# Second attention with 64-column values, transposed heads and an output product of its own

## The chip, the cores and the metric

The kernel runs on one core of one Trainium2 chip. The metric is the device time of one execution in microseconds, median of several runs.

## The reference, cut to what matters

Two layers, each a cross-attention and a feed-forward part, on 32 batches of 128 tokens by 128 features. All four are fused into one kernel. The change is in the second attention:

```
x = x + tanh(g_xattn[1]) * L1_xattn(layernorm(x), ctx)
def L1_xattn(x, context, Wq, Wk, Wv, Wo, bo):      # H = 16 heads, DH = 64
    q = (x @ Wq).reshape(b, n, H, DH)
    k = (context @ Wk * SCALE).reshape(b, m, H, DH)
    v = (context @ Wv).reshape(b, m, H, DH)
    attn = softmax(einsum('bihd,bjhd->bhij', q, k))
    out = einsum('bhij,bjhd->bihd', attn, v).reshape(b, n, H * DH)
    return out @ Wo + bo
```

Behind it a mixture of 8 experts takes each token to the expert with the largest logit (top 1).

## The kernel before, in words

There are five parts, in blocks with a barrier between them: setup, first attention, first FFN, second attention, second FFN. Every instruction of every engine stands in an order written out by hand; engines meet at semaphores. The second attention goes over the 32 batches in a software pipeline: `step(n)` scores and weighs batch n and at the same time projects batch f = n + 1. Batches 0 and 1 are written out, the other 30 are a loop over pairs (`Fori(1, PAIRS)`).

Value and output weights are folded: for each head, `fold` (L789) multiplies Wv of that head (128x64) with Wo of that head (64x128) to a 128x128 matrix, kept in float16 as a high and a low part (`k.M_hi`, `k.M_lo`, written at L683 and L459). In step(n) TensorE does:

- `project` (L1557 to L1566): q and k, four times 12 float16 products of 128 columns into `l_qk_bank`;
- `project_context` (L1568 to L1583): Z = ctx times M, four times three products of 512 columns into `l_tz`; ScalarE copies each to `l_Z` (L1499), where a head has 128 columns and a column of ones;
- `score_by_query` (L1585, tile `l_a`) for the maxima, `transpose_maxima` (L1601), `score_by_key` (L1603, tile `l_b`) for the shifted scores, of which ScalarE takes the exponentials (`l_probs`, L1494);
- `weigh` (L1636 to L1651): eight times two heads, each float32 product with the 128x128 probabilities as the stationary operand and 129 columns of Z moving, into `l_pv`;
- VectorE (`sums`, L1143) takes the reciprocal of the last column and adds each head's 128 columns, scaled, to x or to `l_acc`.
- GpSimd (`pair`, L1432) normalises batch n + 2, adds the bias, makes the low parts of q and k (`rests`, L1424), adds x and `l_acc` to `l_rows` (`rows_out`, L1416) and scatters the rows of two batches to their experts (`scatter`, L1409).

The router's small steps for the pair before (`route_transpose`, `route_logits`, `route_ranks`, `choose`, `put`) lie between these. The bank `l_tz` is one PSUM bank that Z and the transposed x share.

## Time and profile before

| | us |
|---|---|
| median of 3 runs | 820.46 (819.62 to 821.15) |
| the profiled execution's own time | 819.96 |
| its span | 818.2 |
| setup, first attention and first FFN | 0 to 294.5 |
| second attention, from its first product to the last router transposes | 294.5 to 708.5 |
| rest of the routing and second FFN | 708.5 to 818.2 |

The profile is of one execution; 1.8 us of its time lie outside the span. A row of the timeline has a start, a duration, the engine, the line, the operation, and what it writes and reads. Matmuls are pipelined: a duration is a latency, and what a group costs is the distance from its start to the start of the next group. PEld is the load of the stationary operand, PE the product. A float32 product is two instructions, each with a load of its own, so a count of x4 in the weighing is two heads.

### The profile page before, as it was taken

To read this page: it belongs to the slowest core of one execution; us is meant where nothing else is said; L and a number is where in the kernel's file an instruction comes from. 1 tells how busy PE (TensorE), PEld (TensorE's weight loads), DVE (VectorE), ACT (ScalarE), POOL (GpSimd) and SP (SyncE) were. 2 spreads that over 40 slices of the span, in tenths; PEclk is the share of its full clock that TensorE was granted. 3 is DMA by queue.
4 is the path that set the end of the run, shared out by engine and by line. 5 is a ranking of instruction groups with operands and counts; after the bars stand their busy time and mean duration, and the time that the engine had idled before them with its cause. 6 is when DMAs were issued, how large, how long until landed. Compare 5 with 4: busy or idle time off the path is not lost. (4 is left out here: it accounts for less than half of the span.)

```text
span 818.2 us, 30776 instructions
## 1 busy us (share of the span) xinstructions
PE 777.2 (95%) x10683; PEld 637.6 (78%) x10683; DVE 622.3 (76%) x2406; ACT 557.8 (68%) x1125; POOL 475.8 (58%) x892
## 2 busy tenths in 40 slices
PE   3999999999999989999999999999999999979995
PEld 2777777777788858888888888888888888558884
DVE  4799999998777766888888888888888888734442
ACT  1688888886455557777777777777777777447772
POOL 6645777772011155586676776776776776604554
PEclk9999999999999999999999999999999999999998
DMA  8804999800200000000000000000000000023100
GB/s 215 309 3 150 265 246 236 184 1 3 72 1 0 0 1 2 3 7 7 7 0 7 7 7 7 3 3 7 7 7 7 0 7 7 10 67 87 38 30 21
DMA packets 56160, 41.65 MB, mean 51 GB/s; under 512 B 3900, under 2 KB 51654, under 8 KB 55859
## 3 DMA queue, kind: packets, MB, share of 16 engines
q1 hardware_dynamic: 52400, 36.39, 17.6%
q0 software_dynamic: 2272, 4.27, 1.6%
q10 hardware_dynamic: 1440, 0.40, 0.4%
q8 instruction: 27, 0.44, 0.2%
q14 instruction: 21, 0.15, 0.1%
HBM read 18.07 MB, written 23.44 MB: 51 GB/s over the span
## 5 line engine op out<-in xcount | busy, mean ns | idle before, releaser
L1650 PE MATMUL l_pv<-l_Z,l_probs 128*128 128x129 f32 x1024 | 164.1, 284 | 0.5 <-DVE l_acc L1159 0.5
L1650 PEld LDWEIGHTS l_pv<-l_Z,l_probs 128*128 128x128 f32 x1024 | 138.4, 191 | 20.1 <-DVE l_acc L1159 4.9
L1430 POOL TENSOR_TENSOR l_qk_lo<-w,l_qk_hi 128x512 f16<-128x512 f32 x132 | 148.8, 1159 | 0.8 <-ACT l_qk_hi L1510 0.8
L1159 DVE SCALAR_TENSOR_TENSOR x_sb<-l_pv,l_inv,x_sb 128x128 f32 (+1 forms) x256 | 89.8, 351 | 35.3 <-DVE l_inv L1146 6.9
L52 PE MATMUL l_tz<-M,cT 128*128 128x512 f16 x396 | 107.3, 380 | 0.0
L1494 ACT ACTIVATE l_probs<-l_b 128x512 f32<-128x512 f32 x128 | 72.8, 595 | 50.6 <-PE l_b L1616 50.5
L1484 ACT ACTIVATE w<-l_qk_bank 128x512 f32<-128x512 f32 x129 | 77.0, 597 | 43.8 <-PE l_qk_bank L52 42.1
L520 DVE TENSOR_REDUCE n_shared<-fold_bank 128x4 f32<-128x512 f32 x128 | 87.3, 682 | 9.5 <-PE fold_bank L735 9.4
L1136 DVE TENSOR_REDUCE l_neg_max<-l_a 128x4 f32<-128x512 f32 x132 | 85.9, 682 | 2.3 <-PE l_a L1594 1.8
L1488 ACT ACTIVATE l_qk_hi<-w 128x512 f16<-128x512 f32 x129 | 80.5, 624 | 1.0
L1499 ACT ACTIVATE l_Z<-l_tz 128x512 f32<-128x512 f32 x128 | 76.6, 599 | 3.6
L1159 DVE SCALAR_TENSOR_TENSOR l_acc<-l_pv,l_inv,l_acc 128x128 f32<-128x128 f32 x224 | 76.6, 342 | 0.0
L365 POOL TENSOR_TENSOR n_rstd<-n_var,n_half 128x4 f32<-128x4 f32 x20 | 20.2, 1008 | 87.9 <-DVE n_var L359 87.8
L378 POOL TENSOR_TENSOR l_work<-l_stats,l_work 128x1 f32<-128x1 f32 x67 | 12.6, 189 | 79.8 <-DVE l_stats L497 45.6
L1146 DVE RECIPROCAL l_inv<-l_pv 128x2 f32<-128x2 f32 x256 | 40.6, 159 | 20.4 <-PE l_pv L1650 19.9
L52 PE MATMUL l_qk_bank<-cT,w_hi 128*128 (+1 forms) x528 | 55.0, 219 | 0.1
L52 PEld LDWEIGHTS l_tz<-M,cT 128*128 (+1 forms) x396 | 34.5, 98 | 19.8
L52 PE MATMUL l_qk_bank<-l_T_hi,w_hi 128*128 128x128 f16 x268 | 48.7, 220 | 0.2 <-DVE l_T_lo L1130 0.2
L52 PE MATMUL l_qk_bank<-l_T_hi,w_lo 128*128 128x128 f16 x268 | 48.3, 219 | 0.0
L52 PE MATMUL l_qk_bank<-l_T_lo,w_hi 128*128 128x128 f16 x268 | 48.3, 219 | 0.0
L652 ACT ACTIVATE l_stack<-fold_bank 128x512 f16<-128x512 f32 x64 | 39.0, 610 | 13.1 <-PE fold_bank L52 13.1
L52 PE MATMUL l_qk_bank<-cT,w_lo 128*128 (+1 forms) x264 | 47.6, 219 | 0.0
(276 smaller groups left out, 2265.3 us busy)
## 6 DMA issues: line engine op xcount, KB each, us to landing
expert_rows<-empty_row SPq DMA_DIRECT2D x8, 2178.0 KB, 24.4
x_sb<-expert_rows SPq DMA_DIRECT2D x36, 66.0 KB, 2.3
x_sb<-in_x SPq DMA_DIRECT2D x4, 512.0 KB, 6.9
ctx_sb<-in_ctx SPq DMA_DIRECT2D x4, 512.0 KB, 8.2
w<-in_L_ffn_w SPq DMA_DIRECT2D x1, 2048.0 KB, 9.3
w_raw<-in_L_ffn_gate_w SPq DMA_DIRECT2D x1, 1408.0 KB, 9.2
w_raw<-in_L_ffn_up_w SPq DMA_DIRECT2D x1, 1408.0 KB, 11.5
downT<-in_L_ffn_down_w SPq DMA_DIRECT2D x2, 512.0 KB, 4.2
```

The lines of the kernel that those rows point to most:

```text
L52: last = nc.tensor.matmul(out, lhsT, rhs, start=start and n == 0, stop=stop and n == len(pairs) - 1, skip_group_check=True)
L520: nc.vector.tensor_reduce(neg_max[:, s % 2, G * r:G * r + 4], a_bank[r % 2][:, :].rearrange("p (j n) -> p j n", j=4), AX.X, ALU.max, negat ...
L652: nc.scalar.activation(stack[:, s % DEEP, m].rearrange("p j n -> p (j n)"), stack_bank[:, :], ACT.Copy).then_inc(ready, 1)
L1136: nc.vector.tensor_reduce(neg_max[:, at:at + Q], a_bank[half][:, :].rearrange("p (t n) -> p t n", t=Q), AX.X, ALU.max, negate=True).then_i ...
L1146: nc.vector.reciprocal(inv[:, 2 * m:2 * m + 2], O[:, :, P]).then_inc(inv_ready, 1)
L1159: nc.vector.scalar_tensor_tensor(out=total, in0=O[:, h, 0:P], scalar=inv[:, j:j + 1], in1=total, op0=ALU.mult, op1=ALU.add).then_inc(summe ...
L1430: nc.gpsimd.tensor_tensor(qk_lo[:, w, m, Q * u:Q * u + Q].rearrange("p t n -> p (t n)"), qk[:, u, m, :], qk_hi[:, w, m, Q * u:Q * u + Q].r ...
L1484: nc.scalar.activation(qk[:, u, m, :], qk_bank[:, :], ACT.Copy).then_inc(qk_ready, 1)
L1488: nc.scalar.activation(qk_hi[:, w, m, Q * u:Q * u + Q].rearrange("p t n -> p (t n)"), qk[:, u, m, :], ACT.Copy)\
L1494: nc.scalar.activation(probs[:, at:at + Q, :].rearrange("p h n -> p (h n)"), b_bank[half][:, :], ACT.Exp, scale=float(HD1) ** -0.5).then_i ...
L1499: nc.scalar.activation(Z[:, w, Q * q:Q * q + Q, 0:P], tz_bank[:, :].rearrange("p (h n) -> p h n", h=Q), ACT.Copy)\
L1650: last = nc.tensor.matmul(pv_bank[m % 2][:, h * (P + 1):(h + 1) * (P + 1)], probs[:, 2 * m + h, :], Z[:, w, 2 * m + h, :], start=True, sto ...
```

## The change

- Nothing is folded. Wv (columns in another order of heads) and Wo (rows in the same order) are each split by GpSimd into two float16 parts, `k.vo_hi` and `k.vo_lo`, during the first FFN (16 pairs of small operations). The fold's products, copies and subtractions go.
- V = ctx times Wv has 64 columns a head, so that `project_context` runs twice a batch and not four times; `l_V` has 65 columns a head.
- `weigh` runs four times with four heads of 65 columns.
- VectorE divides four heads at once (`sums`, one reciprocal and one product) into a tile `l_heads`.
- New: `transpose_heads`, twice a batch four float32 transposes into `l_tz`; `heads_hi` (ScalarE) and `heads_lo` (VectorE) make float16 parts; `project_heads`, 24 float16 products of 128 columns into `l_qk_bank`; `acc_out` (VectorE) scales the sum.
- The loops are gone, all 32 steps are written out, and the last ones leave out the work for batches that don't exist (the loop did it on padding). In step 0 the maxima are transposed ahead of the first projection. At the start, two results go to banks of their own.
- The routing is spread by `late`, `middle` and `early` over three steps, and `l_rows` and `l_slot_i` have two buffers.

The diff, cut to its core:

```diff
-    for t, name in ((k.wvT, "L1_xattn_Wv"), (k.wo1, "L1_xattn_Wo")):
-        sp.dma_start(t[:, :, :], A[name].rearrange("(j p) n -> p j n", p=P)).then_inc(k.late_landed, 16)
+    sp.dma_start(k.vo_raw[:, 0:H // 2, :].rearrange("p j n -> p (j n)"), A["L1_xattn_Wv"]).then_inc(k.late_landed, 16)
+    sp.dma_start(k.vo_raw[:, H // 2:H, :], A["L1_xattn_Wo"].rearrange("(j p) n -> p j n", p=P)).then_inc(k.late_landed, 16)
...
-                def fold(u):
-                    for t in range(4):
-                        for half in range(2):
-                            some = slice(HD1 * half, HD1 * half + HD1)
-                            last = nc.tensor.matmul(k.fold_bank[2 * u + half][:, t * P:t * P + P], k.wvT[some, 4 * u + t, :], k.wo1[some, 4 * u + t, :],
-                                                    start=True, stop=True, tile_position=(HD1 * half, 0))
-                    last.then_inc(k.folded, 1)
...
+                def split_late(n):
+                    raw, hi, lo = (t[:, bass.ds(n, 1), :].rearrange("p a n -> p (a n)") for t in (k.vo_raw, k.vo_hi, k.vo_lo))
+                    nc.gpsimd.tensor_copy(hi, raw).then_inc(k.vo_hi_ready, 1)
+                    pool.wait_ge(k.vo_hi_ready, n + 1)
+                    nc.gpsimd.tensor_tensor(lo, raw, hi, ALU.subtract).then_inc(k.vo_lo_ready, 1)
...
+                def sums(n, m):
+                    O = pv_bank[m % 2][:, 0:SIDE].rearrange("p (h n) -> p h n", h=Q)
+                    some = slice(Q * m, Q * m + Q)
+                    dve.wait_ge(pv_done, 4 * n + m + 1)
+                    nc.vector.reciprocal(inv[:, some], O[:, :, HD1]).then_inc(inv_ready, 1)
+                    dve.wait_ge(inv_ready, 4 * n + m + 1)
+                    nc.vector.tensor_tensor(heads[:, some, :], O[:, :, 0:HD1],
+                                            inv[:, some].rearrange("p (h a) -> p h a", a=1).broadcast_to([P, Q, HD1]), ALU.mult).then_inc(heads_ready, 1)
+
+                def heads_lo(n, part):
+                    some = slice(Q * part, Q * part + Q)
+                    dve.wait_ge(OT_hi_ready, 2 * n + part + 1)
+                    nc.vector.tensor_tensor(OT_lo[:, some, :].rearrange("p j n -> p (j n)"), tz_bank[:, :],
+                                            OT_hi[:, some, :].rearrange("p j n -> p (j n)"), ALU.subtract).then_inc(OT_lo_ready, 1)
+
+                def acc_out(n):
+                    dve.wait_ge(out_done, n + 1)
+                    dve.wait_ge(x_done, n + 1)
+                    nc.vector.tensor_scalar(acc[:, n % 2, 0:P], qk_bank[:, 0:P], k.tg[:, 1:2], None, ALU.mult).then_inc(acc_ready, 1)
...
-                    for h in range(2):
-                        last = nc.tensor.matmul(pv_bank[m % 2][:, h * (P + 1):(h + 1) * (P + 1)], probs[:, 2 * m + h, :],
-                                                Z[:, w, 2 * m + h, :], start=True, stop=True)
+                    for h in range(Q):
+                        last = nc.tensor.matmul(pv_bank[m % 2][:, h * (HD1 + 1):(h + 1) * (HD1 + 1)], probs[:, Q * m + h, :],
+                                                V[:, n % 2, Q * m + h, :], start=True, stop=True)
                     last.then_inc(pv_done, 1)
+
+                def transpose_heads(n, part):
+                    pe.wait_ge(heads_ready, 4 * n + 2 * part + 4)
...
+                    for t in range(Q):
+                        pair = slice(2 * (Q * part + t), 2 * (Q * part + t) + 2)
+                        last = nc.tensor.transpose(tz_bank[:, t * P:t * P + P], heads[:, pair, :].rearrange("p h n -> p (h n)"), k.ident[:, :])
+                    last.then_inc(OT_moved, 1)
+
+                def project_heads(n):
+                    pe.wait_ge(OT_lo_ready, 2 * n + 2)
+                    if n + 2 < B:
+                        pe.wait_ge(qk_ready, 4 * n + 12)
+                    elif n + 1 == B:
+                        pe.wait_ge(acc_ready, n)
+                    pairs = []
+                    for t in range(H // 2):
+                        hi, lo, w_hi, w_lo = OT_hi[:, t, :], OT_lo[:, t, :], k.vo_hi[:, H // 2 + t, :], k.vo_lo[:, H // 2 + t, :]
+                        pairs += [(hi, w_hi), (lo, w_hi), (hi, w_lo)]
+                    both_products(nc, qk_bank[:, 0:P], pairs).then_inc(out_done, 1)
...
+                def step(n):
+                    f, u, w = n + 1, n % 2, 1 - n % 2
+                    if n == 0:
+                        transpose_maxima(n)
+                    if f < B:
+                        project(f, 1, 0)
+                    if n:
+                        transpose_maxima(n)
+                        weigh(n - 1, 3)
                     score_by_key(n, u, 0)
+                    if f < B:
+                        score_by_query(f, w, 0)
+                        project_context(f, 0)
+                        project(f, 0, 1)
+                    weigh(n, 0)
+                    if n:
+                        transpose_heads(n - 1, 1)
+                    if f < B:
+                        project(f, 1, 1)
+                    weigh(n, 1)
                     score_by_key(n, u, 1)
+                    if f + 1 < B:
+                        transpose(f + 1, u)
+                    if n:
+                        project_heads(n - 1)
+                    if f < B:
+                        score_by_query(f, w, 1)
+                        project_context(f, 1)
+                    if f + 1 < B:
+                        project(f + 1, 0, 0)
+                    weigh(n, 2)
+                    transpose_heads(n, 0)
```

On TensorE, the second half of step 1 stood like this in the kernel before (`l_pv` weighing, `l_b` scores by key, `l_a` scores by query, `l_tz` the shared bank; the twelve products of a projection are left out at the first dots, and after the second ones):

```order
L1650 MATMUL l_pv<-l_Z,l_probs 128x129 x2
L1611 MATMUL l_b<-l_neg_maxT,pick_half 128x128 x8
...
L1616 MATMUL l_b<-l_qk_lo,l_qk_hi 128x128 x8
L1594 MATMUL l_a<-l_qk_hi 128x128 x8
L52 MATMUL l_tz<-M,cT 128x512 x3
L1650 MATMUL l_pv<-l_Z,l_probs 128x129 x2
L52 MATMUL l_qk_bank<-l_T_hi,w_hi 128x128
...
L52 MATMUL l_tz<-M,cT 128x512 x3
L1650 MATMUL l_pv<-l_Z,l_probs 128x129 x2
```

and stands like this in the changed one, up to the end of the step:

```order
L1677 MATMUL l_pv<-l_V,l_probs 128x65 x4
L1631 MATMUL l_b<-l_neg_maxT,pick_half 128x128 x8
...
L1636 MATMUL l_b<-l_qk_lo,l_qk_hi 128x128 x8
L1565 MATMUL l_tz<-ident,l_xn 128x128
L53 MATMUL l_qk_bank<-vo,l_OT_hi 128x128
L53 MATMUL l_qk_bank<-vo,l_OT_lo 128x128
...
L1614 MATMUL l_a<-l_qk_hi 128x128 x8
L53 MATMUL l_tz<-vo,cT 128x512 x3
...
L1677 MATMUL l_pv<-l_V,l_probs 128x65 x4
L1694 MATMUL l_tz<-ident,l_heads 128x128 x4
```

Of the two groups of Z products one is left; the output product of the batch before (24 instructions) and four transposes have come in, and the weighing stands in larger groups. An x2 or x4 of a float32 product here is of heads, two instructions each in the trace.

On GpSimd, the end of a pair stood so in the loop: the scatter of the pair before, then the two additions to `l_rows`.

```order
L1430 TENSOR_TENSOR l_qk_lo<-w,l_qk_hi 128x512
L1396 TENSOR_TENSOR l_taker<-l_taker 128x1
L1414 DMA expert_rows<-l_rows,l_slot_i 35456x132 x2
L1395 ISA
L1396 TENSOR_TENSOR l_taker<-l_taker 128x1
...
L1422 TENSOR_TENSOR l_rows<-x_sb,l_acc 128x132
...
L1422 TENSOR_TENSOR l_rows<-x_sb,l_acc 128x132
```

Now one addition stands ahead of the scatter in an even step, and one in an odd step (an even step and the beginning of the odd one):

```order
L1415 TENSOR_TENSOR l_qk_lo<-w,l_qk_hi 128x512 x2
L1380 TENSOR_TENSOR l_taker<-l_taker 128x1
L1407 TENSOR_TENSOR l_rows<-x_sb,l_acc 128x132
L1380 TENSOR_TENSOR l_taker<-l_taker 128x1
L1398 DMA expert_rows<-l_rows,l_slot_i 35456x132 x2
L1415 TENSOR_TENSOR l_qk_lo<-w,l_qk_hi 128x512 x2
```

Behind the last step the scatter of pair 14 stands ahead of the addition of batch 31 in both.

## Rows read from the trace of the kernel before

**Rows 1.** Page, busy us, share of the span, instructions

```profile
PE 777.2 (95%) x10683; PEld 637.6 (78%) x10683; DVE 622.3 (76%) x2406; ACT 557.8 (68%) x1125; POOL 475.8 (58%) x892
```

**Rows 2.** Busy time by stage: window, length, each engine busy (instructions), granted clock

```profile
320.43:332.26 11.83, 11.83 (x178) 10.20 (x175) 9.39 (x34) 9.25 (x18) 7.12 (x12) 1.00 0.02 4
332.26:344.89 12.63, 12.63 (x183) 10.78 (x181) 10.08 (x42) 9.45 (x18) 7.20 (x13) 1.00 0.01 2
344.89:357.07 12.18, 12.18 (x183) 10.34 (x181) 10.28 (x45) 9.06 (x17) 8.44 (x14) 1.00 0.01 3
357.07:692.21 335.14, 335.14 (x4850) 285.42 (x4848) 276.57 (x1160) 250.07 (x460) 237.06 (x408) 1.00 0.02 6
692.21:708.47 16.26, 14.99 (x189) 11.53 (x186) 12.38 (x53) 10.74 (x19) 10.92 (x20) 1.00 0.03 9
```

**Rows 3.** Timeline of TensorE, batch 1: start, duration, what, count

```profile
320.43 0.28 PE L1601 MATMUL l_a<-ident,l_neg_max 128*128 128x128 f32 x1
320.54 0.61 PE L1650 MATMUL l_pv<-l_Z,l_probs 128*128 128x129 f32 x4
320.99 0.81 PE L52 MATMUL l_tz<-M,cT 128*128 128x512 f16 x3
321.64 0.61 PE L1650 MATMUL l_pv<-l_Z,l_probs 128*128 128x129 f32 x4
322.18 0.40 PE L1611 MATMUL l_b<-l_neg_maxT,pick_half 64*128 64x128 bf16 x8
...
323.08 0.39 PE L1594 MATMUL l_a<-l_qk_hi 64*128 64x128 f16 x8
323.40 0.23 PE L52 MATMUL l_qk_bank<-l_T_hi,w_hi 128*128 128x128 f16 x1
...
324.08 0.66 PE L1650 MATMUL l_pv<-l_Z,l_probs 128*128 128x129 f32 x4
324.58 0.81 PE L52 MATMUL l_tz<-M,cT 128*128 128x512 f16 x3
```

**Rows 4.** Timeline of TensorE, products with 8 moving columns, batches 15 and 16

```profile
492.22 0.48 PE L1627 MATMUL l_pv<-routerT,l_rowsT 128*128 128x8 f32 x3
492.33 0.37 PE L1627 MATMUL l_pv<-routerT,l_rowsT 128*128 128x8 f32 x2
492.56 0.69 PE L1650 MATMUL l_pv<-l_Z,l_probs 128*128 128x129 f32 x4
...
498.61 0.22 PE L52 MATMUL l_pv<-l_onehot,l_ones 128*128 128x8 bf16 x3
498.69 0.69 PE L1650 MATMUL l_pv<-l_Z,l_probs 128*128 128x129 f32 x4
```

**Rows 5.** Waits of weight loads, 320 to 704 us: total, times, longest

```profile
PEld l_pv L1650 <- DVE l_acc L1159: 4.2, 15, 0.3
```

**Rows 6.** Page, groups of instructions: busy, mean ns, idle before

```profile
L1159 DVE SCALAR_TENSOR_TENSOR l_acc<-l_pv,l_inv,l_acc 128x128 f32<-128x128 f32 x224 | 76.6, 342 | 0.0
L1499 ACT ACTIVATE l_Z<-l_tz 128x512 f32<-128x512 f32 x128 | 76.6, 599 | 3.6
```

**Rows 7.** Timeline around the fold, TensorE and VectorE

```profile
199.34 1.16 PE L793 MATMUL fold_bank<-wo,wvT 64*128 64x128 f32 x16
...
205.61 0.74 DVE L459 SCALAR_TENSOR_TENSOR M<-fold_bank,tg,M 128x512 f16<-128x512 f32 x1
```

**Rows 8.** Timeline of TensorE ahead of batch 0

```profile
303.80 0.40 PE L1594 MATMUL l_a<-l_qk_hi 64*128 64x128 f16 x8 [0.27 <-ACT l_qk_hi L1510]
...
309.49 0.28 PE L1601 MATMUL l_a<-ident,l_neg_max 128*128 128x128 f32 x1
```

**Rows 9.** Timeline of GpSimd, last scatter in the loop

```profile
702.67 0.19 POOL L1396 TENSOR_TENSOR l_taker<-l_taker 128x1 f32<-128x1 f32 x1 [1.22 <-DVE l_slot_i L1232]
...
704.74 0.96 POOL L1414 DMA_INDIRECT expert_rows<-l_rows,l_slot_i  x1 [0.30 <-issue]
707.11 0.33 POOL L1396 TENSOR_TENSOR l_taker<-l_taker 128x1 f32<-128x1 f32 x2 [1.40 <-DMA expert_rows<-l_rows,l_slot_i]
```

More of the change, by code:

```diff
@@ L40 @@
 WARM_UP = 8
+HEAD_ORDER = [2 * (4 * u + t) + half for u in range(2) for half in range(2) for t in range(4)]
 SPLIT = 2 * E * I1 + 2 * H * HD1
@@ L1328, in _ @@
+                sums(B - 1, 3)
+                ranks_out(PAIRS - 2)
+                put(PAIRS - 2, 0)
+                heads_lo(B - 1, 1)
+                for part in range(1, 4):
+                    put(PAIRS - 2, part)
+                acc_out(B - 1)
                 j = PAIRS - 1
@@ L1455, in _ @@
                 pool.wait_ge(primed, 6)
-                pool.wait_ge(summed, 4)
+                pool.wait_ge(heads_ready, 2)
                 for u in range(2):
                     bias(u, 4 + u)
-                rests(0, 0, first=True)
-                pair(0)
+                for u in range(2):
+                    rests(0, u, first=True)
+                for n in range(4):
+                    step(n)
                 pool.wait_ge(k.rows_cleared, 16 * (E + 1))
-                pool.wait_ge(row_primed, 1)
-                with pool.Fori(1, PAIRS) as i:
-                    pair(i, i - 1)
+                for n in range(4, B):
+                    step(n)
+                scatter(PAIRS - 2)
+                rows_out(B - 1)
                 deviations(PAIRS - 1)
@@ L1532, in _ @@
-                        z_out(f, w, 2)
+                    for half in range(2):
+                        exponentials(n, 1, half)
+                    if f < B:
+                        v_out(f, 1)
+                    if f + 1 < B:
                         projected(f + 1, 0, 0)
-                        z_out(f, w, 3)
                         projected_hi(f + 1, u, 0, 0)
+                for n in range(B):
+                    step(n)
+                for part in range(2):
+                    heads_hi(B - 1, part)
@@ L1717, in _ @@
+                project_heads(B - 1)
                 pe.wait_ge(exp_done, 4 * B + 4)
```

509 lines of the change are left out of this document (239 added, 270 removed).

## Prediction, made before the changed kernel was run

> **What bounds the kernel now.** Start with the page: TensorE is busy for 95% of the span [rows 1], which may mean little, since its ends are modelled. So the stage the change touches is read next, by windows that run from one transpose of the maxima (L1601) to the next, which is one step of the second attention [rows 2]. A step takes 11.83 us in batch 1, 12.63 and 12.18 in batches 2 and 3, and 335.14 us for the next 27, 12.41 each. In each window TensorE is busy without a gap at the full granted clock, while VectorE is busy for 10.3 us and ScalarE for 9.4 at the most. The waits of the weight loads say the same: the longest kind adds up to 4.2 us over some 380 us [rows 5]. So the second attention goes at the pace at which TensorE can issue, and what is to be priced is the distance from one TensorE group to the next, which is in the timeline of batch 1 [rows 3]:
>
> - a projection of 12 products of 128 columns: 323.40 to 324.08, 0.68 us, mostly 0.67; 0.056 each
> - three products of 512 columns: 320.99 to 321.64, 0.65
> - scores by key 0.90 (322.18 to 323.08), by query 0.32 (to 323.40)
> - a float32 transpose 0.11 (320.43 to 320.54)
> - weighing two heads, four instructions: 0.45 behind other float32 work (320.54), 0.54 ahead of the scores by key (321.64), 0.50 behind a projection (324.08); so 0.112 an instruction, and 0.055 or 0.09 for the change of kind.
>
> With 4 projections (2.68), 4 groups of 512 columns (2.60), 2 of each score (1.81 and 0.64), 2 transposes (0.22) and 8 weighings (3.87) the sum is 11.82, and the trace has 11.83: the price list is complete.
>
> **The weighing.** This is the term on which all rests. The product gets 65 columns for 129. At 129 columns an instruction takes 0.112 us, as much as 258 columns take at 2.4 GHz, so 65 columns would need 0.057. But the stationary operand, 128x128 in float32, is loaded anew for each. The router's product has such an operand and only 8 moving columns: its instructions start at 492.22 and 492.33, and the next group comes at 492.56, two more further on: 0.112 each [rows 4]. The same with a bfloat16 operand takes 0.025 (three from 498.61 to 498.69) [rows 4]. So 0.112 is what the float32 load costs, at 8 as at 129 columns, and I take 0.112 at 65. The bounds are 0.057 and 0.112. The Trainium skill has both sides, on the page "TensorE: Matmul & The Clock Gate": the section "Back-to-back issue gap" lets the moving columns alone set the gap, by which this would come out at the 0.057 bound; the section "LDWEIGHTS (loading the stationary operand)" lets the load take its columns over 1.2 GHz, about 107 ns, whatever moves. The trace sides with the second.
>
> What is left of a gain is the grouping: four groups of 8 instructions at 0.112 are 3.58, with three changes behind a projection (0.165) and two ahead of the scores (0.18) 3.92. Before: 3.87. Nothing is gained.
>
> **The rest of a step.** Z to V takes away two groups of 512 columns: 1.30 off. The heads' transposes are 8 times 0.11: 0.88 on. The output product is 24 times 0.056: 1.34 on. The transpose of x now stands behind the scores by key instead of a weighing; a full-width group behind tiled ones costs more there, some 0.1 to 0.2 (the last gap of scores by query in front of a projection), 0.14 taken. With weighing +0.05 that is +1.11: a plain step of 12.93 us. For the 24 products the page's section "Back-to-back issue gap" also has about 81 ns an instruction in a real stream of loads and products with 128 columns; by it they would cost 0.6 more a step and the sum would be 19 us higher. The twelve in 0.67 say 0.056.
>
> Routing costs TensorE 12.63 - 11.83 = 0.80 in an even step and 0.35 in an odd one [rows 2], 0.57 on average, of which about 0.15 is waiting for VectorE's sums [rows 5]; that wait goes, since VectorE now does a batch's sums in 8 instructions for 24. So 0.42 stays, and a full step takes 13.35 for 12.41.
>
> **Do the others keep up?** ScalarE has two copies of values less and two of transposed heads more, all of 0.60 [rows 6]: the same load. VectorE loses 16 additions of 0.34 [rows 6] and gets two subtractions of 512 columns (0.74 each, as the fold's [rows 7]), four products of 256 columns and one of 128, under 0.74 each: no more than before. The bank `l_tz` is used in turn by V, heads, x, V, heads; with a product 0.65 or 0.45, a copy 0.60 and a subtraction 0.74 and the latencies, the ring is some 8.7 us, inside 13.3. A step walked through from its first projection (0), with TensorE's groups at the distances above: scores by key end at 2.7, so the exponentials are there at 3.5 and 4.0 and `weigh(n, 0)` at 4.3 finds them; the heads transposed at 5.3 to 5.7 are copied by 6.5 and subtracted by 7.3, needed at 8.4 by the transpose of x and at 8.5 by the output product; that one ends at 9.9, `acc_out` at 10.4 at the latest, needed at 10.8 by the projection that takes its bank; ScalarE has the second float16 part of k at 9.5 in a plain step (9.9 with logits, when TensorE is later too), needed at 9.8 by the scores by query; the heads transposed at the end of the step are ready 2.0 into the next, needed at 3.0. So each wait finds its producer done; the tightest margins are 0.2 to 0.4. On GpSimd `rows_out` now comes some 11.4 into each step, just ahead of the router's transposes, and in even steps the scatter (3.0 us) follows it; behind it queue the low parts of q and k for the step after the next, which have a step of slack.
>
> **The steps.** From L1601 of batch 1 to that of batch 31 before: 371.78 us [rows 2]. Now: 12.93, then 13.15 and 13.32 in batches 2 and 3, in which not all routing has begun, 26 steps of 13.35 (347.1), and 11.8 for batch 30, where the projections for a batch that doesn't exist are left out. Together 398.3: +26.5.
>
> **The edges.** (1) The fold goes: two bursts of 1.09 us, 199.34 and again 3.7 us later, hidden for two thirds, and VectorE's subtraction from 205.61 to 206.35 behind which the block ended [rows 7]: -1.4 (0 to -2.5). (2) Ahead of batch 0 the second scores by query start at 303.80 and the maxima are transposed at 309.49 [rows 8], behind two groups of Z, filler products, a second transpose and two projections. In the new order they wait only for VectorE's maxima (two of 0.68), and the first x part comes earlier, as it no longer waits behind the second copy: about 303.7, with the projection that was ahead of it now behind; at the first scores by key this is -5.6 (-4 to -6.5). From there to L1601 of batch 1 the lists before and after have the same length (10.0). (3) At the end: from L1601 of batch 31 to the router's transposes 16.26 before [rows 2]. Now the last weighing is followed by transposes, copy, subtraction, output product and scaling; and GpSimd has the scatter of pair 14 ahead of the last rows, which takes 3.0 us (702.67 to 705.70 [rows 9]). `put` for it is done about 13.9 us in, so the rows are ready at 17.6: +1.4 (0 to +3). (4) GpSimd's 16 splits lie in the first FFN, where it is idle most of each 5 us: 0 (to +2, if they slow VectorE).
>
> **Sum.** 26.5 - 1.4 - 5.6 + 1.4 = +20.9. Against the profiled execution's own 819.96 that is 840.9; this is 0.5 under the median of the runs, and I say 841.
>
> **Rivals.**
> - *The load is no floor* (65 columns take 0.057): 32 instructions times 0.055 are 1.76 a step, 56 us less in all, though ScalarE and VectorE (10 us busy each, in order) would not let a step fall below some 11.6; about 790. For it: the arithmetic of columns. Against it: 8 columns take as long as 129. Below some 0.09 an instruction it would turn the result: 0.02 times 32 times 30 is 21 us. Chance 0.05: faster. The skill's section on the issue gap, quoted above, is this rival's rule.
> - *New waits.* The chain from the transposes through ScalarE and VectorE back to `l_tz`, or `acc_out` before the next projection, comes late by 0.3 to 0.6 a step, as the margins above are only estimates: 30 steps make 9 to 18, so 850 to 859. The same if written-out code had to be fetched late; but batch 1 was written out before, and its step has no gap. Chance 0.13.
> - *Part of the grouping pays more than I count*, and the 0.14 and the routing's 0.2 go too: 0.4 a step less, 829. Chance 0.10.
> - The chance of my own case, 834 to 848, is 0.72.
>
> A measurement tells 0.2% (1.6 us) from no change. Faster: 0.06; within it: 0.01; slower: 0.93. The range that holds 8 in 10: 831 to 851.
>
> **What will show it.** Right: L1601 to L1601 at 13.2 to 13.4 us with TensorE still without gaps; PEld rows of the weighing at 0.112 distance with 65 columns; 24 output products in 1.34; waits of PEld still short. Wrong: weighing instructions closer than 0.1 (first rival); idle time of PEld in front of `l_tz<-ident,l_heads`, `l_qk_bank<-vo` or the projections (second); a first transpose of the maxima later than 305.

## The result: 3 per cent slower, as the price list of TensorE had it

| | before | changed |
|---|---|---|
| median | 820.04 us (819.04 to 821.15, 4 runs) | 844.95 us (841.57 to 848.15, 4 runs) |
| profiled execution | 819.96 us, span 818.2 | 845.78 us, span 844.1 |

The ratio is 1.0305, 95% interval 1.028 to 1.0331. The forecast was 841, range 831 to 851. The two profiled executions differ by 25.8 us. Here is where they lie, each stage between two TensorE instructions that both traces have:

| stage | before | changed | difference | forecast |
|---|---|---|---|---|
| last scores of the first attention to the first hidden product of the first FFN | 11.63 | 11.51 | -0.1 | -1.4 |
| last transpose of that FFN to the first product of the second attention | 2.34 | 3.41 | +1.1 | 0 |
| from there to the transpose of the maxima of batch 1 | 25.90 | 22.04 | -3.9 | -5.6 |
| to that of batch 31 | 371.78 | 396.79 | +25.0 | +26.5 |
| to the router's last transposes | 16.26 | 20.47 | +4.2 | +1.4 |
| all the rest | | | -0.4 | 0 |

The steps make 25 of the 26 us. The four stages that are edges were forecast at -5.6 together and came out at +1.3; the steps were forecast 1.5 too high. Each column is one execution. The end above all differs between profiles: with the same instructions in it (in one of them with fewer moving columns) it takes 19.1, 20.5 and 23.1 us in three of them; run 6 has more on this.

### The profile page after: what moved, and what is told of

It is laid out like the page before. It is cut to its first block and busy times, and to the rows that moved or that the text cites. A ratio compares the mean times of both kernels' runs of the same rounds, so it can differ in the third digit from the quotient of the medians.

```text
span 844.1 us, 29663 instructions
## 1 busy us (share of the span) xinstructions
PE 796.6 (94%) x11374; PEld 677.0 (80%) x11379; DVE 589.0 (70%) x1972; ACT 546.4 (65%) x1107; POOL 481.9 (57%) x907
## 5 line engine op out<-in xcount | busy, mean ns | idle before, releaser
L1677 PE MATMUL l_pv<-l_V,l_probs 128*128 128x65 f32 x1024 | 134.9, 275 | 0.5 <-DVE l_rowsT L1156 0.5
L1677 PEld LDWEIGHTS l_pv<-l_V,l_probs 128*128 128x128 f32 x1024 | 124.4, 192 | 0.7 <-issue 0.7
L1497 ACT ACTIVATE l_OT_hi<-l_tz 128x512 f16<-128x512 f32 x64 | 38.2, 597 | 39.6 <-PE l_tz L1694 38.4
L1140 DVE TENSOR_TENSOR l_heads<-l_pv,l_inv 128x256 f32<-128x256 f32 x128 | 54.3, 424 | 4.4
L53 PE MATMUL l_tz<-vo,cT 128*128 128x512 f16 x192 | 52.5, 383 | 0.0
L53 PE MATMUL l_qk_bank<-cT,w_hi 128*128 128x128 f16 x504 | 52.5, 219 | 0.0
L53 PE MATMUL l_qk_bank<-vo,l_OT_hi 128*128 128x128 f16 x512 | 49.4, 222 | 1.4 <-DVE l_OT_lo L1146 1.4
L1146 DVE TENSOR_TENSOR l_OT_lo<-l_tz,l_OT_hi 128x512 f16<-128x512 f32 x64 | 43.9, 685 | 9.2 <-ACT l_OT_hi L1497 7.1
L1897 POOL DMA_INDIRECT out<-f_result,f_token x39 | 38.5, 988 | 13.9 <-issue 10.2
L53 PE MATMUL l_qk_bank<-vo,l_OT_lo 128*128 128x128 f16 x256 | 45.6, 222 | 0.0
## 6 DMA issues: line engine op xcount, KB each, us to landing
w_raw<-in_L_ffn_up_w SPq DMA_DIRECT2D x1, 1408.0 KB, 11.6
```

What stands on the lines that cost most here:

```text
L53: last = nc.tensor.matmul(out, lhsT, rhs, start=start and n == 0, stop=stop and n == len(pairs) - 1, skip_group_check=True)
L1140: nc.vector.tensor_tensor(heads[:, some, :], O[:, :, 0:HD1], inv[:, some].rearrange("p (h a) -> p h a", a=1).broadcast_to([P, Q, HD1]), AL ...
L1146: nc.vector.tensor_tensor(OT_lo[:, some, :].rearrange("p j n -> p (j n)"), tz_bank[:, :], OT_hi[:, some, :].rearrange("p j n -> p (j n)"), ...
L1677: last = nc.tensor.matmul(pv_bank[m % 2][:, h * (HD1 + 1):(h + 1) * (HD1 + 1)], probs[:, Q * m + h, :], V[:, n % 2, Q * m + h, :], start=T ...
L1897: nc.gpsimd.indirect_dma_start(out, bass.IndirectOffsetOnAxis(token[:, p, v:v + 1], 0), result[:, p, v, :], None, bounds_check=last_row, o ...
```

## The profile after

The page's first line, the answer to [rows 1]:

```profile
PE 796.6 (94%) x11374; PEld 677.0 (80%) x11379; DVE 589.0 (70%) x1972; ACT 546.4 (65%) x1107; POOL 481.9 (57%) x907
```

VectorE lost 33 us of work and TensorE got 19 more. Only the second shows in the time. The windows that answer to [rows 2], from one transpose of the maxima to the next: window, length, busy time of PE, PEld, DVE, ACT and POOL, granted clock:

```profile
304.68:317.12 12.44, 11.20 (x176) 9.63 (x177) 5.42 (x15) 9.44 (x19) 7.93 (x12) 1.00 0.01 1
317.12:329.99 12.87, 12.87 (x204) 11.57 (x202) 7.60 (x20) 9.20 (x18) 7.25 (x13) 1.00 0.01 2
329.99:343.02 13.03, 13.03 (x205) 11.73 (x203) 7.87 (x22) 9.19 (x18) 7.40 (x13) 1.00 0.01 3
343.02:356.36 13.34, 13.34 (x207) 12.05 (x205) 9.85 (x33) 9.20 (x18) 7.91 (x15) 1.00 0.01 2
356.36:713.91 357.55, 357.55 (x5528) 322.21 (x5526) 256.66 (x802) 246.44 (x456) 237.34 (x398) 1.00 0.02 7
713.91:734.38 20.47, 16.77 (x185) 13.66 (x185) 9.43 (x39) 6.04 (x10) 5.47 (x11) 0.83 0.04 14
```

From batch 1 to batch 31 TensorE has no gap, at the full clock, and no wait of a product or of a weight load is in the list of waits, that of [rows 5] neither. A full step takes 13.34 and 13.25 us by turns. Batch 0 (first row) and the end (last row) do have gaps, and at the end the clock is 0.83. TensorE in batch 1, as in [rows 3]: start, latency, line, operation, count:

```profile
317.12 0.28 PE L1621 MATMUL l_a<-ident,l_neg_max 128*128 128x128 f32 x1
317.24 1.00 PE L1677 MATMUL l_pv<-l_V,l_probs 128*128 128x65 f32 x8
318.18 0.40 PE L1631 MATMUL l_b<-l_neg_maxT,pick_half 64*128 64x128 bf16 x8
...
320.73 1.06 PE L1677 MATMUL l_pv<-l_V,l_probs 128*128 128x65 f32 x8
321.62 0.61 PE L1694 MATMUL l_tz<-ident,l_heads 128*128 128x128 f32 x4
322.06 0.22 PE L53 MATMUL l_qk_bank<-cT,w_hi 128*128 128x128 f16 x1
...
324.89 0.22 PE L53 MATMUL l_qk_bank<-vo,l_OT_hi 128*128 128x128 f16 x1
...
326.32 0.40 PE L1614 MATMUL l_a<-l_qk_hi 64*128 64x128 f16 x8
```

Weighing four heads is eight instructions, and the next group comes 0.89 us after the first of them (320.73 to 321.62), or 0.94 ahead of the scores (317.24 to 318.18): 0.112 each with 65 columns, as with 129 [rows 3] and with 8 [rows 4]. The loads of the stationary operand follow one another at the same distance:

```profile
317.13 0.98 PEld L1677 LDWEIGHTS l_pv<-l_V,l_probs 128*128 128x128 f32 x8
```

Four transposes of heads take 0.44 (to 322.06). The 24 output products stand 0.056 apart (median), 1.43 us with the change to the scores by query behind them (324.89 to 326.32).

## Experiments

Runs 1 to 4 share a chip, runs 5 to 8 a second and runs 9 to 12 a third. Ratios are to the kernel before, run on that same chip. On the second chip the second FFN took 11.5 us longer in each of the four profiles (108.5 for 97.0 in the changed kernel's), and the kernel before took 831.8 us, so those four are read by stages. Of the kernel before there is no profile on that chip.

**1. Fewer columns.** Is it the load?

```
-  last = nc.tensor.matmul(pv_bank[m % 2][:, h * (HD1 + 1):(h + 1) * (HD1 + 1)], probs[:, Q * m + h, :],
-                          V[:, n % 2, Q * m + h, :], start=True, stop=True)
+  last = nc.tensor.matmul(pv_bank[m % 2][:, h * (HD1 + 1) + HD1 // 2:(h + 1) * (HD1 + 1)], probs[:, Q * m + h, :],
+                          V[:, n % 2, Q * m + h, HD1 // 2:], start=True, stop=True)
...
-  awake(2)
+  awake(1)
+  keep_awake(nc, k, pv_bank[1], 1)
```

The second edit sends one of two fillers at the start into the other bank.

> The changed kernel, but each weighing instruction moves 33 of the 65 columns (the lower half of each head's output is left stale, so the output is another). Theory: the float32 stationary operand's load is the floor, so a weighing instruction stays at 0.112 us, a full step at 13.3 us and the kernel at its time, 842 to 848. Rival: the columns that move set the distance in part; 32 columns less at 0.055 us an instruction would be 1.76 us a step and 54 us in all, about 791; if only half of that, about 818.

846.13 us, ratio 1.0346 (1.0319 to 1.0373). The columns halved once more, and the kernel did not get faster. A full step takes 13.26 and 13.19 us, 0.08 and 0.06 less than in the changed kernel. In its timeline, one weighing group and what follows:

```profile
398.65 1.06 PE L1677 MATMUL l_pv<-l_V,l_probs 128*128 128x33 f32 x8
399.55 0.63 PE L1694 MATMUL l_tz<-ident,l_heads 128*128 128x128 f32 x4
```

Eight in 0.90 us, 0.112 each. From 129 moving columns down to 33 the distance stays.

**2. The same products in 16 bits.** Column count and place unchanged, only the type:

```
-  V = sb("V", [P, 2, H, HD1 + 1])
-  probs = sb("probs", [P, H, P])
+  V = sb("V", [P, 2, H, HD1 + 1], F16)
+  probs = sb("probs", [P, H, P], F16)
```

> The changed kernel with the probabilities and the values in float16 instead of float32 (less precise), the instructions and the columns as they were. Theory: with the float32 load gone a weighing instruction costs what 65 columns or a 16-bit load cost, 0.027 to 0.056, so TensorE's part of a step falls by 1.8 to 2.7 us; ScalarE (9.2 us busy a step) and VectorE (9.6) then come near, a step takes 11.0 to 11.6 us and the kernel 780 to 795. Rival (0.112 is what any instruction of this group costs, for its place between other work or its destination): no change, 842 to 848.

781.95 us, ratio 0.9552 (0.9522 to 0.9581): 7 per cent under the changed kernel. The weighing, two such groups of TensorE's timeline with what follows, and the second scores by query with theirs:

```profile
623.66 0.29 PE L1677 MATMUL l_pv<-l_V,l_probs 128*128 128x65 f16 x4
623.94 0.63 PE L1694 MATMUL l_tz<-ident,l_heads 128*128 128x128 f32 x4
...
639.00 0.40 PE L1614 MATMUL l_a<-l_qk_hi 64*128 64x128 f16 x8
640.08 0.82 PE L53 MATMUL l_tz<-vo,cT 128*128 128x512 f16 x3 [0.68 <-DVE l_T_lo L1121]
```

Four heads are four instructions for eight, at 0.032 us for 0.112 (median distance inside a group). So float32 was the floor. Both operands changed their type here. That of the two it is the load of the stationary one follows from the distance staying at 0.112 with 8, 33, 65 and 129 moving columns; no run changes the type of one operand alone. A step takes 10.84 and 11.74 us by turns; in the longer one the products for V wait for the low part of x. VectorE and GpSimd show what delays it:

```profile
638.70 1.12 DVE L1192 TENSOR_TENSOR l_equal<-l_equal,l_less 128x16 f32<-128x16 f32 x1
639.75 0.28 DVE L1121 TENSOR_TENSOR l_T_lo<-l_tz,l_T_hi 128x128 f16<-128x128 f32 x1
...
638.64 1.15 POOL L1415 TENSOR_TENSOR l_qk_lo<-w,l_qk_hi 128x512 f16<-128x512 f32 x1 [0.58 <-ACT l_qk_hi L1481]
```

A product of 16 columns, which takes 0.16 us in the changed kernel (median of L1192; 1.12 here), ends when GpSimd's subtraction beside it ends (639.8), and the low part of x stands behind it. This is a second bound, that the float32 load had covered.

**3. A third of the output product.** Is TensorE's issue the only bound?

```
-  pairs += [(hi, w_hi), (lo, w_hi), (hi, w_lo)]
+  pairs += [(hi, w_hi)]
```

> The changed kernel with 8 of the 24 products of the output projection (the two low-part terms are left out, so it is less precise); their operands are still made. Theory: TensorE's issue is the only bound, so each of the 16 products takes 0.056 us away, 0.90 us a step: a full step 12.40 us, the kernel 28 us faster, about 817. Rival: the low part of the heads, ScalarE's and VectorE's chain or the bank is just as late as TensorE now, and the gap that opens is filled by a wait: gain under 15 us, with idle time of TensorE ahead of the output product or the projections.

832.84 us, ratio 1.0165 (1.0139 to 1.019): 11.5 us saved, where 28 were expected. A full step is 12.95 us. The rival was right that a wait fills the gap and that the gain stays under 15 us, but not in the place: TensorE waits neither for the heads nor for the bank. The list of waits has one new entry (total, times, longest), and TensorE's and ScalarE's timelines show the place:

```profile
PEld l_a L1614 <- ACT l_qk_hi L1481: 16.5, 27, 0.6
```

```profile
637.92 0.61 PE L53 MATMUL l_qk_bank<-vo,l_OT_hi 128*128 128x128 f16 x8
638.97 0.40 PE L1614 MATMUL l_a<-l_qk_hi 64*128 64x128 f16 x8 [0.44 <-ACT l_qk_hi L1481]
...
638.12 0.28 ACT L1471 ACTIVATE l_T_hi<-l_tz 128x128 f16<-128x128 f32 x1 [1.22 <-PE l_tz L1565]
638.29 0.62 ACT L1481 ACTIVATE l_qk_hi<-w 128x512 f16<-128x512 f32 x1
```

The scores by query want the second float16 copy of the keys. It stands on ScalarE behind the copy of the transposed x, which idles 1.22 us for a transpose that TensorE does just before the output product. From the eighth product to the scores are 0.66 us for 0.06. The 24 products had covered this. The margin of 0.2 to 0.4 that the prediction gives this wait is about what it was: 16 products are 0.90 us, and a step fell by only 0.3 to 0.4; the other 0.5 to 0.6 went into the wait.

**4. Written out, alone.** The kernel before with Python loops in place of the four engine loops of the second attention.

> The kernel before, with the loops of its second attention written out and nothing else changed: the same instructions in the same order. Theory: written-out code costs nothing, since its fetches run ahead: 820 within 1 us, and TensorE's distances from step to step as before (12.41 us on average). Rival: the fetches (several times the bytes of the loop's) come late at places, or take the place of the loops' own cost: 1 to 10 us slower with gaps of TensorE that are in no wait, or up to 2 us faster, as the branches between the passes go.

819.86 us against 818.73, ratio 1.0019 (1.0002 to 1.0035): at the edge of what can be told. Both theories have a part. Steps are 12.55 and 12.09 us, where the loops give 12.64 and 12.17 (the same in run 10, on another chip), so each is 0.08 shorter; but six steps are longer by 0.2 to 0.5. In the list of waits TensorE has two entries for routing transposes and transposes of x that the loops' trace hasn't (total, times, longest):

```profile
PEld l_tz L1550 <- POOL l_xn L383: 1.3, 4, 0.3
PEld l_pv L1622 <- DVE x_sb L1159: 1.1, 2, 0.6
```

So now and then GpSimd and VectorE were late. From batch 1 to 31 it comes out even: 371.71 for 371.78. The Trainium skill (page "Runtime: NRT & Kernel Launch", section "Instruction fetch mechanics") holds that straight code is fetched ahead and that a taken branch can stall. The 0.08 is no such stall: set side by side, the two traces have the same distances on TensorE from the end of one pass to the start of the next, and the loop's 0.16 us lies in four weighings inside the pass, 0.03 to 0.06 in each. What it is stays open. Whether a late fetch stands behind the six longer steps no run shows.

**5. ScalarE's order.** Run 3 with the copies of ScalarE exchanged:

```
+  projected_hi(f, w, 1, 1)
   transposed_hi(f + 1)
-  projected_hi(f, w, 1, 1)
```

> The run with 8 output products, and in each step ScalarE's second float16 copy of the keys moved ahead of its copy of the transposed x. In the run without the move TensorE had one gap of 0.66 us a step, ahead of the second scores by query, which wait for that copy; the copy stood behind the transposed x's, which waits for a transpose that TensorE does only just before. Theory: the output product of 24 had covered this wait, and with the order changed the gap goes: a step 0.55 to 0.6 us shorter (12.35 for 12.95), the kernel about 815. Rival: the gap is the length of ScalarE's own work (two projections, the copies), so the same gap stays, 833, or it moves to the products behind T's low part.

Ratio 1.0113 (1.0084 to 1.0142), where run 3 had 1.0165: 4 us for the 17 expected. Half of the steps took 12.35 us, exactly the theory's; the other half 13.36, longer than before. In those the wait moved, as the rival had it in its last words. TensorE, VectorE and GpSimd:

```profile
635.25 0.82 PE L53 MATMUL l_tz<-vo,cT 128*128 128x512 f16 x3 [0.85 <-DVE l_T_lo L1121]
...
632.07 1.15 DVE L1190 TENSOR_TENSOR l_equal<-l_logits,l_best 128x16 f32<-128x16 f32 x1
633.14 0.15 DVE L1169 TENSOR_SCALAR l_row_var<-l_row_stats 128x2 f32<-128x2 f32 x1
633.21 1.15 DVE L1170 TENSOR_SCALAR l_row_mean<-l_row_stats 128x2 f32<-128x2 f32 x1
...
632.03 2.31 POOL L1415 TENSOR_TENSOR l_qk_lo<-w,l_qk_hi 128x512 f16<-128x512 f32 x2 [1.32 <-ACT l_qk_hi L1481]
```

With the copy earlier, GpSimd's two subtractions follow one another directly (2.31 us), and two of VectorE's smallest instructions sit out one each. For L1190 that is nothing new (median 1.141 us in the changed kernel and in run 3); L1170 has a median of 1.149 us here and 0.155 in run 3. The Trainium skill (page "SBUF — State Buffer", section "SBUF: two separate sides") says that VectorE, with two SBUF inputs or in a two-port mode, and GpSimd take one pair of ports as an exclusive lock for a whole instruction; the trace agrees for L1190, which has two SBUF inputs, with a wait as long as GpSimd's subtraction (1.157). L1170 has one input, and in which mode it ran the trace does not show.

**6 and 7. The end.** The changed kernel with fillers in the waits behind the last weighing (6); in 7 also the last rows ahead of a scatter:

```
   weigh(B - 1, 3)
+  keep_awake(nc, k, b_bank[0], 5)
   transpose_heads(B - 1, 1)
+  keep_awake(nc, k, b_bank[0], 7)
   project_heads(B - 1)
-  pe.wait_ge(exp_done, 4 * B + 4)
-  keep_awake(nc, k, b_bank[0], 10)
+  keep_awake(nc, k, b_bank[0], 5)
```

```
+  rows_out(B - 1)        # run 7 alone
   scatter(PAIRS - 2)
-  rows_out(B - 1)
```

First the end of the changed kernel itself, TensorE, then GpSimd:

```profile
726.00 0.66 PE L1694 MATMUL l_tz<-ident,l_heads 128*128 128x128 f32 x4 [0.91 <-DVE l_heads L1140]
728.06 0.29 PE L53 MATMUL l_qk_bank<-vo,l_OT_hi 128*128 128x128 f16 x1 [1.41 <-DVE l_OT_lo L1146]
...
731.02 3.52 PE L243 MATMUL l_b<-pick_half 128*128 128x512 bf16 x9 [0.22 <-issue]
734.38 0.38 PE L1642 MATMUL l_pv<-ident,l_rows 128*128 128x128 f32 x2
...
729.33 1.04 POOL L1398 DMA_INDIRECT expert_rows<-l_rows,l_slot_i  x1 [0.49 <-issue]
730.67 0.96 POOL L1398 DMA_INDIRECT expert_rows<-l_rows,l_slot_i  x1 [0.30 <-issue]
731.66 0.20 POOL L1380 TENSOR_TENSOR l_taker<-l_taker 128x1 f32<-128x1 f32 x1
```

Within the second wait the granted clock falls to its lower level, 1.2 GHz, and stays there from 727.0 to 733.9. The output product takes 2.5 us for 1.34 and a filler 0.43 for 0.216; all ten fillers (nine have a row in the trace) stand in front of the router's transposes (734.38), though the rows were there at 732.3.

> The changed kernel with filler products in the two long waits behind the last weighing (5 and 7 of 0.216 us) in place of 5 of the 10 that stood behind the last output product. Theory: TensorE's clock stays at 2.4 GHz there, the output product takes 1.34 us for 2.5 and the fillers behind it 0.216 each, so the router's transposes start 18.4 to 18.7 us after the maxima's last transpose for 20.5: 1.8 us less, though the rows still wait for GpSimd, which is in the scatter of the pair before. Rival: the clock falls in any case, or the fillers themselves hold the transposes of the heads up: 20 or more.

> The same fillers, and on GpSimd the last rows' addition put ahead of the scatter of pair 14, which took 3.0 us and ended at the moment at which the addition started. Theory: the router's transposes start 16.8 to 17.5 us after the last transpose of the maxima, 1.1 to 1.6 less than with fillers alone: of the 4.2 us that the end lost against the kernel before, the clock was about half and this order a third. Rival: the scatter started later is waited for by the last slots or by the loads at the end, and what is won at the transposes is lost there: no gain against the fillers alone.

Ratios 1.0299 (1.0274 to 1.0323) and 1.0277 (1.025 to 1.0304). The stage that took 20.47 us takes 18.42 in run 6, where the clock stays at 2.4 GHz, and 16.88 in run 7: both inside what the theory had. By themselves the ratios are no proof.

How much the fillers give back depends on the profile that run 6 is held against. Run 8 and run 1 have the end of the changed kernel unchanged but for the moving columns of run 1, with the same two waits. In run 8 the clock is low from 727.0 to 730.4 alone, and the stage takes 19.12 us. In run 1 it is low from 715.4 to 722.2 and from 725.6 to 732.4, and the stage takes 23.12. So the fillers are worth 0.7 us against run 8 (on the same chip), 2.0 against the changed kernel's own profile and 4.7 against run 1. The 1.54 us between runs 6 and 7 have the full clock on both sides. In 6 TensorE has its fillers done and waits for GpSimd, in 7 no longer:

```profile
736.03 0.44 PE L1642 MATMUL l_pv<-ident,l_rows 128*128 128x128 f32 x2 [1.66 <-POOL l_rows L1407]
```

```profile
730.46 1.24 PE L243 MATMUL l_b<-pick_half 128*128 128x512 bf16 x5
731.82 0.44 PE L1642 MATMUL l_pv<-ident,l_rows 128*128 128x128 f32 x2
```

The transposes to the first product of the second FFN take 15.63 and 15.73 us (16.18 in the changed kernel, 15.66 in run 8), so the gain is not given back.

**8. The start.** Three edits in the changed kernel: in the last steps of the first attention four fillers where the fold's products had been; GpSimd's splits one group earlier; ScalarE's exchange of run 5 in batch 0 alone (the lines below show the first two).

```
+  if n in (B, B + 1): keep_awake(nc, k, k.fold_bank[0], 4)
-  split_late(m * E + e)
+  if e == 0: split_late(m * E)
+  if e < E - 1: split_late(m * E + e + 1)
```

> The changed kernel with three edits ahead of batch 1: fillers in the two places of the first attention's last steps where the fold's products stood; GpSimd's sixteen splits one group earlier each, so that the last group has none; in batch 0 alone ScalarE's second float16 copy of the keys ahead of its copy of the transposed x. Theory: the clock no longer falls at the start of the feed-forward (0.8 us), the second attention begins 0.6 to 1.1 us earlier, and step 0 takes 11.3 to 11.7 us for 12.44: together the transpose of the maxima of batch 1 comes 2.2 to 2.9 us earlier. Rival: these are hidden elsewhere (the feed-forward is paced by its own chain of 5 us a group, the batch-0 stall moves to the values' product, which waits for the low part of x): under 1 us.

Ratio 1.0286 (1.0259 to 1.0313), by itself no proof, but the stages are plain. From the last scores to the first hidden product: 10.35 us, where the six other runs of the changed kernel's design without these fillers (1 to 3, 5 to 7) have 11.4 to 11.6. The clock in that stretch, changed kernel and run 8 (window, length, busy times, clock):

```profile
205.32:209.73 4.41, 4.41 (x18) 2.58 (x17) 1.42 (x4) 1.07 (x2) 0.00 (x0) 0.67 0.87 297
```

```profile
204.99:208.40 3.41, 3.24 (x17) 1.81 (x16) 1.41 (x4) 1.24 (x2) 0.00 (x0) 1.00 0.77 251
```

From the FFN's last transpose to the second attention: 2.57 us for 3.41 (3.58 in runs 5 to 7, on the same chip as run 8). In the changed kernel the last thing that ended before it was GpSimd's split:

```profile
292.65 1.01 POOL L364 TENSOR_TENSOR n_rstd<-n_var,n_half 128x4 f32<-128x4 f32 x1 [3.16 <-DVE n_var L358]
293.62 0.29 POOL L885 CAST vo<-vo_raw  x1
294.09 0.42 POOL L887 TENSOR_TENSOR vo<-vo_raw,vo  x1 [0.18 <-POOL vo L885]
...
295.08 0.38 PE L243 MATMUL l_pv<-pick_half 128*128 128x512 bf16 x1 [3.14 <-PEq L838]
```

Batch 0 took 11.92 us for 12.44, half of what was expected. In batch 0 there is no output product yet, so run 3's wait stands in the changed kernel itself:

```profile
313.46 0.40 PE L1614 MATMUL l_a<-l_qk_hi 64*128 64x128 f16 x8 [0.89 <-ACT l_qk_hi L1481]
```

With the exchange it is gone, but 0.36 us of waiting for the low part of x stand ahead of the products for V, as the rival had it. A wait of 0.35 ahead of the first scores by query is in both.

Together, from the last scores of the first attention to the maxima's transpose of batch 1 (without the middle of the FFN): 35.8 us in run 8, 38.1 and 38.0 in runs 6 and 7, 37.0 in the changed kernel's own profile. So 2.2 to 2.3 us on the same chip, as expected, but only 1.15 against the changed kernel's profile, in which the clock does not fall at the start of the second attention as it does in runs 6 to 8.

**9. The kernel before with 16 bits.** The types of run 2, applied to the probabilities and Z:

> The kernel before with its probabilities and its values times output weights (129 columns a head) in float16 instead of float32 (less precise), nothing else. Theory: here too the float32 load goes and with it half the instructions: 16 of about 0.054 us (129 columns) in place of 32 of 0.112, 2.7 us less of TensorE a step. But VectorE's sums are 10.3 us busy in a step of 11.8, in a fixed order, and become the bound: a step 10.6 to 11.3 us, the kernel 5 to 6.5 per cent faster than before, as fast as the changed kernel with the same (4.5 per cent). Rival: VectorE is near 12 us with its waits, and the gain is under 2 per cent: then keeping the values apart pays only with 16-bit operands.

793.36 us, ratio 0.9685 (0.9654 to 0.9717). A step takes 11.6 us, and TensorE now waits (first the window over most of the steps, then the longest entries of PEld's waits):

```profile
372.00:660.00 288.00, 253.31 (x4053) 186.90 (x4053) 256.26 (x1066) 223.79 (x422) 216.21 (x375) 1.00 0.02 6
```

```profile
PEld l_pv L1650 <- DVE l_acc L1159: 16.7, 37, 0.6
PEld l_tz L1550 <- issue: 14.2, 13, 1.1
PEld l_pv L1622 <- POOL l_rows L1422: 12.5, 13, 1.1
```

VectorE is busier than TensorE (256.3 to 253.3 of 288), and it ends the waits of 35 us of the 68 in that list. GpSimd ends most of the others: its rows 12.5, and the transposes of x, "issue" above, stand in PE's own list as 12.0 behind GpSimd's normalised x. So the theory named one of two engines; steps took 11.6, not 10.6 to 11.3, and the gain is 3.2 per cent, not 5 to 6.5. So with 16-bit operands the design with the values kept apart is the faster one, 0.9552 for 0.9685, and with float32 it is the slower.

**10 and 11. What of the change pays alone.** The kernel before with the changed kernel's batch 0 (10); and with the loops written out and the missing batch's work left out too (11).

```
   awake(3)
+  transpose(0, 0, first_T[0])
+  project(0, 1, 1, first=0, bank=b_bank[1])
   ...
+  if first: transpose_maxima(n)
   project(f, 1, 0)
```

> The kernel before with batch 0 in the changed kernel's way alone: the transposes of x into a bank of the scores, the projections in two banks by turns, the maxima first. Theory: this part of the change is worth its 4.5 to 5.5 us by itself, as its first maxima transpose comes 5 us earlier and its batch 0 has no new wait (the transpose of x stands far ahead of the scores): 0.5 to 0.7 per cent faster. Rival: the time is given back before batch 1, as the values' four groups for batch 0 now stand between: under 2 us, 0.2 per cent.

813.76 us, ratio 0.9921 (0.9901 to 0.9941). From the first product of the second attention to the maxima's transpose of batch 1: 21.55 us for 25.90, 4.35 less, just under the 4.5 to 5.5 expected. This part of the change is a gain by itself.

> The same, with the loops written out and the work for a batch that does not exist left out of the last step, as the changed kernel has it (6.0 us of TensorE). Theory: the last step is then paced by the exponentials and by VectorE's sums, and the router's transposes start 12.5 to 14 us after the last maxima for 16.3: together 0.9 to 1.1 per cent faster than before. Rival: VectorE's sums or GpSimd's rows set the end already, and only 1 us comes of it: 0.6 per cent, with TensorE's clock falling at the end.

814.06 us, ratio 0.9913 (0.9889 to 0.9937): not to be told from 10. The last interval fell from 12.63 to 11.88 and the end from 16.26 to 15.31, 1.7 us, while the expectation had 2 to 4 for the end alone. TensorE is done and waits for GpSimd's rows, which stand behind the scatter of the pair before, as they did in run 6:

```profile
703.05 0.44 PE L1638 MATMUL l_pv<-ident,l_rows 128*128 128x128 f32 x2 [1.43 <-POOL l_rows L1429]
```

The clock fell only behind that (1.2 GHz from 704.7 to 708.1). That the 1.7 us don't show in the medians has no cause that was tested: five of the written-out steps are longer, as in run 4, and before the first FFN's first hidden product the profiles of this case differ by up to 4.2 us (207.4 to 211.6), run 11's being 3.7 us later there than run 10's. The rival was right: GpSimd's rows set the end.

**12. All together, with 16 bits.** Runs 2, 7 and 8, ScalarE's exchange in every step, and seven fillers at the end of the first FFN:

> The changed kernel with float16 probabilities and values and all that the other runs found: fillers at the start of the feed-forward, at its end and at the end of the second attention, GpSimd's splits one group earlier, the last rows ahead of the scatter, and ScalarE's second copy of the keys ahead of that of x in every step. Theory: 4.5 per cent from the float32 load, as measured, 4 us from the end, 2 to 3 from the start: 5.3 to 5.6 per cent faster than before. Rival: with TensorE no longer the only bound, the new order of ScalarE's copies decides: if the low part of x comes late by it, each step loses up to 0.4 us, 12 in all, and it is slower than the float16 run alone.

775.23 us, ratio 0.9446 (0.9422 to 0.947): 8.3 per cent under the changed kernel, and faster than both. The clock is at 2.4 GHz from 30.9 to 768.2 us, the end takes 13.90 us and batch 0 10.72. ScalarE's exchange gave nothing in the steps (10.84 and 11.77 us, as in run 2), as VectorE's low part of x is still what TensorE waits for (12.4 us in 14 waits from 330 to 640). What each of the parts adds here was not tried. This kernel and run 2 round probabilities and values to float16, which the other two don't.

## Why the prediction was right, step by step

- *TensorE's issue bounds the steps.* Right for both kernels: no gap in 30 steps.
- *The float32 load is the floor, 0.112 at 65 columns.* Right, and now shown from both sides: no change at 33 columns (run 1), 0.032 in 16 bits (run 2), with the reserve given at run 2. The Trainium skill's section "LDWEIGHTS (loading the stationary operand)" (page "TensorE: Matmul & The Clock Gate") gave 107 ns, and 112 were measured; but with the same 128 columns in 16 bits the products stood 32 ns apart, so its time does not set the distance there. The formula by columns alone in the Trainium skill's section "Back-to-back issue gap" (same page) is stated there for an isolated product, and the section itself says that in a stream loads and products both set the distance. It gives 0.030 us for 65 columns; the prediction's 0.057 counts a float32 column as two.
- *A step.* 12.93 forecast and 12.87 measured for batch 1; 13.35 and 13.30 for a full one. The output product took 0.056 an instruction, not the 0.081 that the Trainium skill's section "Back-to-back issue gap" (page "TensorE: Matmul & The Clock Gate") gives for a stream. Over the 30 steps the forecast was 1.5 us too high.
- *Every wait finds its producer done, margins 0.2 to 0.4.* Right for batches 1 to 30, though by no more than it said: run 3 opened a wait with 0.90 us less of TensorE. For batch 0 it was wrong (edge 2).
- *Edge 1, the fold's end, -1.4.* The time was won (run 8: -1.3), but the changed kernel had -0.1: where the fold's products had been TensorE now waits, its clock falls, and the first products of the FFN run at 1.2 GHz. The step costed what was removed and not what its removal does to the clock.
- *Edge 2, the start, -5.6.* Measured -3.9. At the first scores by key 5.3 of the 5.6 were there. What failed is that from there on the lists have the same length (10.0): it took 10.08 us before and takes 11.50 now. Two waits for ScalarE's float16 copies (0.35 and 0.89) are 1.24 of the 1.42; the walk through a step that found each producer done has an output product in it, and batch 0 has none.
- *Edge 3, the end, +1.4.* Measured +4.2. GpSimd's scatter was there as said, but the clock was not in the sum. Against this profile fillers take back 2.0, and the order on GpSimd 1.5 more. As the clock falls for longer or shorter in the same end, the stage was +2.9 in run 8's profile and +6.9 in run 1's; the 4.2 is one draw.
- *Edge 4, the splits in idle time, 0.* They cost 0.8 to 1.1 (1.0 on the second chip), not by slowing VectorE but because the last of them ends the block. One group earlier, most of that is gone.

The errors of the edges, +1.3, +1.1, +1.7 and +2.8, add up to 6.9; with -1.5 in the steps and -0.4 in the rest that is 5.0, but for rounding the distance from 840.9 to the profiled execution's 845.8. All four edges came out slower than forecast. The number held since the steps, 25 of the 26 us, were priced right, not since the edges were.

One product in the first rival is off: 0.02 times 32 times 30 is 19 us, not 21. Nothing hangs on it.

## What to carry to other kernels

Price a matmul by its stationary operand first: to make the moving side narrower gained nothing here while a 128-column float32 load took 0.112 us, and the type was worth more than the layout. Where work is taken off TensorE at a stage's edge, look at what the clock does in the gap that it leaves; a few filler products there returned 1.1 us ahead of the FFN and, by the profile that they are held against, 0.7 to 4.7 at the end. A stage that shows no wait can still have one just covered: take a covering product out and look, before you count on its time.

## What the runs showed of the hardware beyond that

- TensorE's granted clock fell to 1.2 GHz at three edges, beside the setup (between 17 and 35 us, in most profiles) and the last 5 to 8 us of all. Ahead of the first FFN it fell in a gap of 1.0 us, with gaps of 0.7, 0.3, 0.7 and 0.4 in the 6 us before (in the kernel before, gaps of 0.3, 0.4 and 1.3 there did not lower it); at the end in a gap of 1.4 behind one of 0.9. At the start of the second attention it fell in the profiles of runs 3 and 5 to 8, behind 2.6 to 3.6 us without new work, and not in those of the changed kernel and of runs 1, 2 and 9 to 11, behind 2.6 to 3.4. There, in run 6, the clock was 0.52 from 297.13 to 300.10, and the first projection and the first products for V took 2.5 us for 1.3.
- The same end of the kernel, with the same gaps, had the lower clock for 3.4 us in run 8, 6.9 in the changed kernel and 6.8 twice in run 1, so that one profile doesn't give what such a gap costs.
- In run 9 the clock fell in the middle of the steps (355.9 to 359.3), with waits of 0.75 and 0.93 us for GpSimd in the 4 us before, and that step took 13.59 us for 11.6.

- VectorE instructions of 2 or 16 columns took 1.15 us beside a GpSimd subtraction of 1.16.
- A pass of a loop over two batches cost TensorE some 0.16 us against written-out code, none of it where one pass meets the next (run 4), and written-out code gave it back in six longer steps.
